# A new slot order in the middle stage of a four-engine attention kernel, and free TensorE products in three waits

## What is computed

```python
q = jnp.einsum('bsd,ed->bse', x, Wq).reshape(bsz, seqlen, HQ, D)
k = jnp.einsum('bsd,ed->bse', x, Wk).reshape(bsz, seqlen, HK, D)
v = jnp.einsum('bsd,ed->bse', x, Wv).reshape(bsz, seqlen, HK, D)
q = _rope(_rmsnorm(q, q_norm_w), pos)
k = _rope(_rmsnorm(k, k_norm_w), pos)
k_all = jnp.concatenate([kc, k], axis=1)       # 512 cached keys and 128 new ones
v_all = jnp.concatenate([vc, v], axis=1)
scores = jnp.where(valid, jnp.einsum('bqhd,bkhd->bhqk', q, k_all) * SCALE, -1e+30)
probs = jax.nn.softmax(scores, axis=-1)
o = jnp.einsum('bhqk,bkhd->bqhd', probs, v_all).reshape(bsz, seqlen, HQ * D)
return jnp.einsum('bse,de->bsd', o, Wo)
```

## Time and profile before

| what | value |
|---|---|
| time, median of 3 runs | 1282.56 us (1281.14 to 1286.61) |
| the profiled execution: its own time, its span | 1286.0 us, 1284.2 us |
| TensorE busy | 1193.3 us, 93% of the span |
| VectorE, ScalarE, GpSimd busy | 973.6, 848.6, 968.9 us |
| granted TensorE clock, mean | 0.978 of full |
| middle stage | from about 250 to about 1240 us |

### The profile page before, as it was taken

How to read it: one execution, slowest core, us unless ns; L and a number is a source line. 1 busy time by engine, 2 the same in 40 slices (tenths; PEclk the granted TensorE clock), 3 DMA queues, 4 the chain that set the end, 5 groups by cost and what they waited for, 6 DMA issues and landing times.

```text
span 1284.2 us, 23898 instructions
## 1 busy us (share of the span) xinstructions
PE 1193.3 (93%) x6856; PEld 1003.8 (78%) x6856; DVE 973.6 (76%) x2388; ACT 848.6 (66%) x2441; POOL 968.9 (75%) x723
## 2 busy tenths in 40 slices
PE   6799997699999999998999999989998999999988
PEld 4577775578888878787888778878887888788778
DVE  3477856568787878787878788877887788778876
ACT  2677776566767667676766676667676777666741
POOL 1656656487888798888887988798879877987862
PEclk9899998999999999999999999999999999999999
DMA  7556554256665666566656565656665666556651
GB/s 262 199 186 235 217 219 153 68 120 157 143 141 134 154 142 145 121 151 138 140 127 147 130 159 120 158 128 145 148 158 120 142 146 141 132 131 135 152 148 66
DMA packets 336036, 191.32 MB, mean 149 GB/s; under 512 B 149153, under 2 KB 320162, under 8 KB 334882
## 3 DMA queue, kind: packets, MB, share of 16 engines
q1 hardware_dynamic: 334896, 189.63, 58.2%
q10 hardware_dynamic: 1010, 0.17, 0.1%
HBM read 101.66 MB, written 37.75 MB: 109 GB/s over the span
## 4 chain that ended last, share of the span: by engine, by line
PE 57%; POOL 22%; DMA 6%; issue 5%; ACT 4%; DVE 3%; SPq 3%; DVEq 0%; POOLq 0%; ACTq 0%
PE ps L1290 10%; PE ps L1292 10%; PE ps L1291 10%; POOL b_p_l L1731 9%; DMA b_moved<-b_blk_first 5%; PE ps L1358 4%; POOL b_w_l L1689 3%; SPq L1254 3%; PE ps L1351 3%; PE ps L1350 3%; PE ps L247 3%; ACT b_p_h L1493 2%; PE ps L1318 2%; PE ps L259 2%; PE ps L306 2%
## 5 line engine op out<-in xcount | busy, mean ns | idle before, releaser
L1731 POOL TENSOR_TENSOR b_p_l<-b_moved,b_p_h 128x1280 fp32r<-128x1280 f32 x128 | 379.1, 2962 | 86.9 <-ACT b_p_h L1493 86.9
L1591 DVE CUSTOM_DVE_ANT_0 b_sm<-ps,mask_row,b_rstd 128x640 f32<-128x640 f32 x256 | 223.0, 871 | 54.1 <-PE ps L1292 53.4
L1487 ACT ACTIVATE b_sm<-b_sm,b_mn 128x640 f32<-128x640 f32 x256 | 212.2, 829 | 76.3 <-DVE b_mn L1591 69.7
L1493 ACT ACTIVATE b_p_h<-b_moved 128x1280 fp32r<-128x1280 f32 x128 | 163.4, 1276 | 86.0 <-DMA b_moved<-b_blk_first 82.5
L1620 DVE SCALAR_TENSOR_TENSOR b_hacc<-ps,b_ri,b_hacc 128x512 f32<-128x512 f32 x248 | 182.7, 737 | 5.2 <-PE ps L1292 4.8
L1290 PE MATMUL ps<-b_w_h,x1t_h 128*128 128x512 f32 (+1 forms) x512 | 184.1, 360 | 1.0 <-DVE b_qt_l L1578 0.8
L1291 PE MATMUL ps<-b_w_l,x1t_h 128*128 128x512 f32 (+1 forms) x512 | 178.1, 348 | 0.0
L1292 PE MATMUL ps<-b_w_h,x1t_l 128*128 128x512 f32 (+1 forms) x512 | 177.1, 346 | 0.0
L1290 PE MATMUL ps<-b_kt_h,b_qt_h 128*128 128x320 f32 x512 | 163.4, 319 | 1.5 <-DVE b_mn L1591 1.5
L1291 PE MATMUL ps<-b_kt_l,b_qt_h 128*128 128x320 f32 x512 | 158.2, 309 | 0.0
L1292 PE MATMUL ps<-b_kt_h,b_qt_l 128*128 128x320 f32 x512 | 157.8, 308 | 0.0
(11 more groups left out here) (174 smaller groups left out, 3175.9 us busy)
## 6 DMA issues: line engine op xcount, KB each, us to landing
b_moved<-b_blk_first SPq DMA_DIRECT2D x256, 160.0 KB, 3.3
b_moved<-b_blk_second SPq DMA_DIRECT2D x256, 160.0 KB, 3.1
kv_of_batch<-in_kv SPq DMA_DIRECT2D x128, 256.0 KB
b_ck<-kv_of_batch SPq DMA_DIRECT2D x64, 256.0 KB, 4.3
b_cv<-kv_of_batch SPq DMA_DIRECT2D x256, 64.0 KB, 2.6
raw<-in_w SPq DMA_DIRECT2D x32, 384.0 KB, 4.8
raw<-in_wo SPq DMA_DIRECT2D x32, 256.0 KB, 4.2
a_xt<-in_xt SPq DMA_DIRECT2D x8, 256.0 KB, 6.3
```

Source lines behind the costliest of these rows:

```text
L1487: act.activation(sm[:, h % 2], sm[:, h % 2], ACT.Exp, bias=mn[:, m.b % 2, h:h + 1], scale=-1.0, accum_out=rs[:, m.b % 2, h:h + 1]).then_in ...
L1493: act.activation(pair_of(p_h, pair), moved_pair(pair), ACT.Copy).then_inc(mh_sb, 1)
L1591: dve.tensor_tensor_reduce(sm[:, h % 2], score_row(h), mask_row[:, m.b], rstd[:, m.b % 4, h:h + 1], -MASKED, ALU.add, ALU.min, mn[:, m.b % ...
L1731: pool.tensor_tensor(pair_of(p_l, pair), moved_pair(pair), pair_of(p_h, pair), ALU.subtract).then_inc(ml_sb, 1)
```

## The change

Three things change. First, the order inside a middle-stage slot on TensorE, VectorE, ScalarE and GpSimd: `values_of_lows(last)` now stands after `project_q(two)`, `project_kv(two)` ahead of `scores(one, 0)` and both ahead of `out(last, 0)` and `out(last, 1)`; the other engines' lists are rearranged too, with the squares split three and one, `rope_queries` ahead of `low_probs(m, 0)`, and the weights moved to the slots b = 5 (queries), 6 (key and value) and 1 (output; their loads one slot earlier). Second, the banks of the four output products alternate (OT, SM, OT, SM). Third, TensorE multiplies the identity by a weight tile into the free bank PT at three places of the first batch: four products ahead of `turn_k(0)`, two each ahead of `turn_probs(0, 3)` and `turn_probs(0, 6)`. Their results are overwritten.

```diff
@@ -160,6 +160,8 @@
         def inside(b):
             return 0 <= b < B
+        SPARE = {(0, 3): 2, (0, 6): 2}
+
         def context_bank(b):
             return M2 if inside(b + 2) else M0
@@ -224,6 +226,11 @@
             store(B - 1)
         def run_tensor(pe, ahead):
+            def keep_busy(n):
+
+                for _ in range(n):
+                    pe.matmul(ps[:, PT, :], ident[:], wq[:, 0, 0:D], start=True, stop=True)
+
             def low_rank(a):
                 if a == 0:
@@ -270,6 +277,8 @@
             def turn_k(a):
+                if a == 0:
+                    keep_busy(4)
                 pe.wait_ge(rope_keys_done, a + 1)
                 wait(pe, cxl_sb, a - 1)
                 flat = kr[:].rearrange("p g j d -> p (g j d)")
@@ -300,8 +309,9 @@
                             mm.then_inc(sc_ps, 1)
             def turn_probs(b, c):
+                wait(pe, pt_sb[(c + 1) % 2], 4 * b + (c + 1) // 2)
+                keep_busy(SPARE.get((b, c), 0))
                 pe.wait_ge(pn_sb, 8 * b + c + 1)
-                wait(pe, pt_sb[(c + 1) % 2], 4 * b + (c + 1) // 2)
                 for j in range(4):
                     mm = pe.transpose(ps[:, PT, j * P:(j + 1) * P], pr[:, c % 4, j], ident[:])
                 mm.then_inc(pt_ps, 1)
@@ -1119,7 +1129,7 @@
         sem = lambda n: ctx.enter_context(nc.semaphore("b_" + n))
         (sync_first, tensor_first, scalar_first, vector_first, gpsimd_first), (xl_sb, x1_out) = first_stage
         SC, OT, SM, PJQ, PJK = (0, 2), 4, 5, 6, 7
-        OUT = (SM, OT, OT, SM)
+        OUT = (OT, SM, OT, SM)
         NK = NT * P
         CUT = NK // 2
         LEAD = 512 - CUT
@@ -1258,8 +1268,8 @@
                 blocks_across(m, 1)
                 if two:
                     key_rows(two)
-                if m.b in (2, 3, 4, 5):
-                    chunk(m.g + 1, m.b - 2)
+                if m.b in (1, 2, 3, 4):
+                    chunk(m.g + 1, m.b - 1)
                 if m.b in (6, 7) and m.g + 1 < G:
                     chunk(m.g + 1, KT + m.b - 6)
                 if m.b == 0 and m.g > 0:
@@ -1367,8 +1377,8 @@
                     wait(pe, h_sb, REP * m.n)
                 if m.b == 0:
                     pe.wait_ge(wol_sb, KT * m.g + h + 1)
-                if h == 2:
-                    pe.wait_ge(h_sb, REP * m.n + 2)
+                if h > 1:
+                    pe.wait_ge(h_sb, REP * m.n + h - 1)
                 tile = slice(h * P, (h + 1) * P)
                 three(ps[:, OUT[h], :], (o_h[:, tile], o_l[:, tile]), (wo_h[:, h], wo_l[:, h])).then_inc(wo_ps, 1)
@@ -1386,22 +1396,23 @@
                 scores(m, 3)
                 if last:
                     values_of_highs(last)
-                    values_of_lows(last)
                 if one:
                     turn_new(one)
                 if two:
                     project_q(two)
+                if last:
+                    values_of_lows(last)
                 if m.n == end.n:
                     gate_rows(pe, 0)
                 if m.n == end.n - 1:
                     turn_rows(pe, 0)
+                if two:
+                    project_kv(two)
+                if one:
+                    scores(one, 0)
                 if last:
                     out(last, 0)
                     out(last, 1)
-                if one:
-                    scores(one, 0)
-                if two:
-                    project_kv(two)
                 if m.n == end.n - 1:
                     turn_rows(pe, 1)
                 if m.n == end.n:
@@ -1441,12 +1452,13 @@
                 wait(act, wo_ps, REP * (B * g - 1) + c + 1)
                 act.activation(wo_h[:, c], raw[:, c, 0:D], ACT.Copy).then_inc(woh_sb, 1)
-            def squares(m):
+            def squares(m, heads=range(REP)):
                 act.wait_ge(qab_sb, m.n + 1)
                 wait(act, rstd_sb, m.n)
-                for h in range(REP):
+                for h in heads:
                     op = act.activation(squares_out[:, h], ps[:, PJQ, h * P:(h + 1) * P], ACT.Square, accum_out=ss[:, h:h + 1])
-                op.then_inc(qsq_sb, 1)
+                if h == REP - 1:
+                    op.then_inc(qsq_sb, 1)
             def new_kv(m):
@@ -1511,38 +1523,39 @@
                     h_out(act, 1)
                 if one:
                     queries(one)
+                    cache_keys(one)
+                if m.b == 1:
+                    out_weights(m.g, 0)
+                    out_weights(m.g, 1)
+                exponent(m, 2)
+                if one:
+                    turned_key(one)
                 if m.b == 6:
-                    q_weights(m.g + 1, 2)
-                    q_weights(m.g + 1, 3)
-                if one:
-                    cache_keys(one)
+                    kv_weights(m.g + 1)
+                exponent(m, 3)
                 if m.b == 1:
                     out_weights(m.g, 2)
                     out_weights(m.g, 3)
-                exponent(m, 2)
-                if m.b == 6:
-                    kv_weights(m.g + 1)
                 if one:
-                    turned_key(one)
-                exponent(m, 3)
-                if last:
-                    output(last)
-                if one:
+                    cache_values(one)
                     new_keys(one)
-                    cache_values(one)
-                high(m, 0)
-                if m.n == end.n - 1:
-                    h_out(act, 0)
-                if two:
-                    squares(two)
-                if m.b == 0:
-                    out_weights(m.g, 0)
-                    out_weights(m.g, 1)
                 if m.b == 5:
                     q_weights(m.g + 1, 0)
                     q_weights(m.g + 1, 1)
+                if last:
+                    output(last)
+                if m.b == 5:
+                    q_weights(m.g + 1, 2)
+                    q_weights(m.g + 1, 3)
+                if m.n == end.n - 1:
+                    h_out(act, 0)
+                high(m, 0)
+                if two:
+                    squares(two, range(REP - 1))
                 if one:
                     exponent(one, 0)
+                if two:
+                    squares(two, range(REP - 1, REP))
             scalar_first(act, (q_weights, kv_weights, squares, new_kv, queries, turned_key, cache_keys, new_keys, cache_values))
             slots(act, slot)
@@ -1624,6 +1637,8 @@
             def slot(m, one, two, last):
                 before = last.before() if last else None
+                if before:
+                    accumulate(before, 1)
                 turn_blocks(m, 0)
                 minima(m, 1)
                 if before:
@@ -1632,18 +1647,15 @@
                     new_values(one)
                 minima(m, 2)
                 turn_blocks(m, 1)
+                if one:
+                    queries(one)
                 if before:
                     accumulate(before, 3)
                 if m.n == end.n:
                     h_rest(dve, 1)
                 minima(m, 3)
-                if one:
-                    queries(one)
                 turn_blocks(m, 2)
                 turn_blocks(m, 3)
-                if last:
-                    output(last)
-                    invert(last)
                 if one:
                     new_keys(one)
                 if m.n == end.n - 1:
@@ -1651,11 +1663,12 @@
                 if two:
                     rope_products(two)
                 if last:
-                    accumulate(last, 0)
+                    output(last)
+                    invert(last)
                 if one:
                     minima(one, 0)
                 if last:
-                    accumulate(last, 1)
+                    accumulate(last, 0)
             def low_weights(g, c):
@@ -1670,6 +1683,7 @@
             vector_first(dve, (rope_products, new_values, queries, new_keys, minima, low_weights, low_kv_weights))
             slots(dve, slot)
+            accumulate(end.before(), 1)
             accumulate(end.before(), 2)
             accumulate(end.before(), 3)
             choose(dve, 0)
@@ -1733,29 +1747,30 @@
             def slot(m, one, two, last):
                 if one:
                     rms(one)
+                    key_sum(one)
+                if m.b == 6:
+                    low_probs(last, 0)
                 if last:
                     low_probs(last, 1)
-                if one:
-                    key_sum(one)
                 if m.b == 6:
-                    q_weights(m.g + 1, range(2, KT))
+                    kv_weights(m.g + 1)
                 if one:
                     cache_keys(one)
                 if m.b == 1:
+                    out_weights(m.g, 0)
+                    out_weights(m.g, 1)
                     out_weights(m.g, 2)
                     out_weights(m.g, 3)
-                if m.b == 6:
-                    kv_weights(m.g + 1)
                 if one:
                     cache_values(one)
-                low_probs(m, 0)
```

(9 more changed lines are left out.)

## The result

The changed kernel takes 1340.65 us (median of 4 runs, 1338.31 to 1341.54), the kernel before, on the same chip, 1283.75 us (4 runs, 1281.14 to 1286.61). The ratio is 1.044, with a 95% interval of 1.041 to 1.047: slower, by 57 us between the medians and by 52.3 us between the spans of the two profiled executions (1336.5 against 1284.2).

The account below looks back on a forecast made before the run. TensorE was taken as the bound: 873.6 us of work in sixty slots of 929.0, 55.4 in holes. Middle stage +45.9, slot n = 1 +1.8, free products -3.9: +43.8 on 1284.2, so 1328, or 1326 against the median; range 1314 to 1338.

Parts of the forecast that it names:

- the clock rival: Middle stage, slots b = 6: the clock falls 8 to 15 times at 1.7 us each, 1340 to 1352; chance 0.13.
- The loop in every slot: Lows, ScalarE cached values and new keys, VectorE new keys, `project_kv`: starts at 1.58 instead of 0.23; 1.46 us a slot.
- b = 6: Middle-stage slots where GpSimd's low probabilities come late: 1.5 us of wait, 1.6 with the slower first pass, seven times.
- b = 1: Middle-stage slots where two output weights stand ahead of `turned_key` on ScalarE: 0.35 us each, seven times.
- The clock: Clock falls after waits, a risk in the middle stage: nothing put in the sum.
- Outside the sixty slots: Slot n = 1 adds 1.8 us, first-stage free products save 3.9, the last two slots add nothing.
- slot n = 1: Middle-stage slot ahead of the first row of the sixty: adds its own 1.8 us.
- The pairs of free products: First stage: take 1.8 us in waits of 2.92, about the same time; put at 0.
- Span to median: Span forecast 1328; the profiled execution lies 3.4 above the median of 1282.56, so 1326 against that median.
- The gain arrives: Rival: no loop in the middle stage, slots stay at 14.6, -39.3, about 1240; chance 0.06.
- Only the output product waits: Rival: `project_kv` isn't held, the hole is 0.9 and a slot 15.5, +14.7, about 1295; chance 0.05.
- nothing changes: Rival: hole and gain cancel, so the time stays the same; chance 0.02.

Follow-up runs that it names:

- run 1: Changed kernel with `new_keys(one)` put ahead of `cache_values(one)` on ScalarE: 1273.1 us, 0.994 of the kernel before.
- run 2: Changed kernel, order untouched, with a third buffer for the high part of the cached values: 1244.9 us, 0.971 of the kernel before.
- run 4: Changed kernel with the output copy put ahead of `cache_values` and `new_keys` on ScalarE: 1364.2 us, 1.063 of the kernel before.
- run 3: Changed kernel with `scores(one, 0)` put ahead of `project_kv(two)` on TensorE: 1356.8 us, 1.058 of the kernel before.
- run 8: Changed kernel with new keys ahead of cached values, plus eight free products ahead of the lows product in b = 6 slots: 1262.1 us, 0.984 of the kernel before.
- run 10: First batch's free products alone, added to the kernel before: 1278.6 us (0.997); taken out of the changed kernel: 1342.7 us (1.045).
- run 9: Changed kernel with the third buffer, VectorE instead of GpSimd splitting one query weight and the key and value weights: 1242.8 us, 0.969 of the kernel before.
- 6: Changed kernel with the lows product alone put back ahead of the turned key and query projection on TensorE: 1336.0 us, 1.041 of the kernel before.
- run 5: Kernel before, old order, with only a third buffer for the high part of the cached values: 1283.1 us, 1.001 of the kernel before.

## Why the prediction was right, point by point

The sign, the mechanism and the range of 1300 to 1350 held. The forecast of 1326 was 15 us short, and the measured 1340.7 lies just above its own range (1314 to 1338). It lies in the range that the clock rival had (1340 to 1352), but that rival didn't come true as it was put: three falls, not 8 to 15. Each step:

- **The loop in every slot: right, 0.09 us too short.** Worked out: 1.58 from the last lows pass to `project_kv`; measured: 1.67. The links were 0.50, 0.53, 0.29 and 0.35, against 0.44, 0.52, 0.31 and 0.31. The release from TensorE to ScalarE and that from VectorE to TensorE were each some 0.05 under-sized. The slot grew by 1.53 instead of 1.46: 4.2 us over sixty. Runs 1 and 2 show that the loop is the cause, run 4 that its length goes to the slot one to one, and run 3 that it is the new keys, not the place of `project_kv`, that TensorE waits for.
- **b = 6: right in the seven slots that split weights.** +1.54 (1.6 worked out): waits for p_l of 1.27 on the average of seven ((12.9 - 4.0) / 7). The terms as worked out give 11.75 + 15.4 - 16.02 = 11.13 and not 11.25, so 1.4 of wait and not 1.5. The key and value weights were just hidden, as said, and became the next wait when the loop was opened (runs 1, 2 and 8).
- **b = 1: right,** +0.28 for 0.35; a slot with b = 3 in the first group took 0.28 more too, and no term had it.
- **The clock: the term of the sum that was set wrong.** I put nothing, and the rival had 8 to 15 falls. There were three in seven b = 6 slots: 1.56 + 1.52 + 1.33 = 4.4 us. A fourth, behind the last b = 6 slot, lies outside the sixty. With the loop's 4.2 and some -0.6 from b = 6 and b = 1 that makes the sixty slots +54.0 instead of +45.9.
- **Outside the sixty slots:** -2.1 worked out, -1.7 measured, and part of that agreement is luck. The free products gave some 3.5 us of the 3.9, and an earlier first projection the other 0.4. The +1.8 of slot n = 1 came (first highs pass of item 1 to that of item 2: 16.37 against 14.56). For the last two slots I put nothing, and there the change lost 2.0 (53.2 - 50.3 at the marks of items 61 and 62, then -0.9 to the end). Slot n = 62 has b = 6 and no query projection ahead of its lows product, so the move gives p_l no more time, while GpSimd has put pair 0 off:

```profile
1271.22 1.96 PE L1368 MATMUL ps<-b_p_l,b_v_h 128*128 128x512 f32 x4 [3.99 <-POOL b_p_l L1745]
```

In the kernel before this wait is 2.1 us:

```profile
1218.91 1.20 PE L1358 MATMUL ps<-b_p_l,b_v_h 128*128 128x512 f32 x4 [2.08 <-POOL b_p_l L1731]
```

- **The pairs of free products: right.** The first pair, which I let run in 1.8 us, ran partly at half clock (3.47 us for four instructions at 45.63; 1.98 in the kernel before with the products, run 10), and it cost nothing: from the stage's first projection to the first `project_kv` it is 199.3 us in the one and 199.2 in the other.
- **Span to median.** The span was off by 8.5 us, the median by 14.7. The kernel before was profiled in an execution 3.4 above its median of three runs (2.3 above that of four), the changed one in an execution 2.3 below. Only the profiled ones have a trace; I can't say what the others lost.
- **The rivals.** "The gain arrives" was the faster one, on condition that the loop isn't there: run 2 takes the loop away and gives 1244.9, against the 1240 worked out for it. "Only the output product waits" and "nothing changes" fell with the wait of `project_kv` in each slot. The rule that was weighed (the Trainium skill, "TensorE: Matmul & The Clock Gate", section "A second HAM failure mode: psum-queue depth-cycling") would have the regular hole cost clock: here it does not, at 1.27 us in 16.1, nor at 1.47 (run 3) or 1.70 (run 4); the clock stayed at 1.00 after every hole of an ordinary slot.

## What to carry to other kernels

Before you move an instruction later, list who waits for its semaphore through buffer reuse, walk on from each of them along its engine's queue until you are back at the engine where you started, and compare the walk with the work that now stands between: the difference is paid in every iteration, even by an engine that is 90% busy. Do the walk through every engine, GpSimd's queue too; in the two runs where I followed only one loop, I missed by 60 and 93 us. Here one more buffer or two exchanged lines on ScalarE opened the loop. The edits of one reordering can be bad apart (1336 without the move of the lows, 1433 with that move alone) and good together with the missing buffer (1245).

## What the runs showed of the hardware

**Which waits cost the clock.** The table takes the seven slots b = 6 of each run that split weights; a fall is a stretch of windows that reach 0.5 to 0.6 right behind the waits.

| run | waits in b = 6, us | falls in 7 |
|---|---|---|
| 9 | 0.76 and 0.6 | 0 |
| 2 | 0.7 and 1.0 | 1 |
| changed kernel, and without the free products (10) | 1.3 and 1.27 | 3 and 3 |
| 4 | 1.3 and 1.7 | 3 |
| 1 | 1.8, and 1.0 in four | 6 |
| 3 | 1.1 and 2.2 | 7 |
| 8 | filled, then 1.0 | 0 |
| 6 | 3.9 | 7 |
| kernel before, run 5, kernel before with the free products (10) | 1.9 to 2.2 alone | 3, 2 and 1 |

A single hole of 1.27 us in a slot never did it, and neither did one of 1.47 (run 3) or 1.70 (run 4). A wait of 0.5 us more (1.8 for 1.3, runs with two waits close together) took the falls from three to six. But the length of a wait alone doesn't decide: with single waits of 1.9 to 2.2 us in the b = 6 and b = 1 slots, the clock fell in 6, 4 and 5 of 14 (kernel before, run 5, kernel before with the products), and run 8 has one of 2.8 us at 1195.50, behind its free products, with no fall. What decides is not shown. A fall cost up to 3.4 us (18.8 us lost in the seven of run 1), and a free bank with a few useless products in the wait took it away. Nor is a fall always paid: in the kernel before a b = 6 slot with one and the slot behind it take 33.4 us together (from 461.94), those without one 33.5 (from 586.79), because the wait of 1.4 us for the turned queries in the second slot is gone.

**VectorE beside GpSimd.** The 128x1024 subtraction on VectorE took 3.19 us in run 9, and the same shape takes 1.19 us at 212.61 in the first stage of the changed kernel, most of it beside a GpSimd instruction that started 0.1 us later. That GpSimd instruction took 1.99 us, where most of its line (L747) take 1.04. In the fence of run 9 the subtraction started while GpSimd's instruction ran and ended 1.1 us after that one's end (582.27 to 583.36); the next one on GpSimd then took 2.27 instead of the 1.32 it has in the changed kernel. So the two take turns, and do not share. The Trainium skill, "SBUF — State Buffer", section "Who interferes with whom", states this rule: a VectorE instruction with two SBUF inputs contends with a GpSimd instruction that reads SBUF, and the contention is "an exclusive lock", so that the order of issue decides who waits. The trace agrees, with the numbers above. So work that is moved from a busy GpSimd to VectorE in this form is paid on both: here VectorE was held 2.0 us longer, and GpSimd lost 0.95 of the 2.40 that it was to save.
